# Attention after a group norm: TensorE's side work cut into single matmuls and laid out anew over the sixteen slots of each head

## What is computed

```python
x = x + conv_ref(gn(x), Wq, Wk, Wv, Wproj, bproj)
# conv_ref: q, k, v = xs @ Wq[h], xs @ Wk[h], xs @ Wv[h]
# att = softmax(q @ k.T / 8);  out = att @ v, heads side by side;  out @ Wproj + bproj
```

## Time and profile before

| | |
|---|---|
| median of 3 runs | 4953.66 us (4952.3 to 4955.85) |
| span of the profiled execution | 4946.9 us, 6.8 us under that median |
| TensorE busy | 4705.1 us (95%), 20608 instructions |
| VectorE, ScalarE, GpSimd busy | 2775.5, 2886.6, 2326.6 us |
| mean granted TensorE clock | 0.994 |

### The profile page before, as it was taken

How to read it: one execution, slowest core, us unless ns; L and a number is a source line. 1 busy time by engine, 2 the same in 40 slices (tenths; PEclk the granted TensorE clock), 3 DMA queues, 4 the chain that set the end, 5 groups by cost and what they waited for, 6 DMA issues and landing times.

```text
span 4946.9 us, 73065 instructions
## 1 busy us (share of the span) xinstructions
PE 4705.1 (95%) x20608; PEld 3505.4 (71%) x20608; DVE 2775.5 (56%) x5284; ACT 2886.6 (58%) x5507; POOL 2326.6 (47%) x1837
## 2 busy tenths in 40 slices
PE   7999999999999999999999999999999999999998
PEld 5777767777676776767767677676776767767675
DVE  5655646556465564655646556465564655646454
ACT  4665646556465564655646566464664646656465
POOL 2444545445454454544545445454444545445455
PEclk9999999999999999999999999999999999999999
DMA  2111111111111111111111111211112111111101
GB/s 69 34 37 55 31 53 35 46 46 32 52 34 50 43 34 54 31 53 41 32 54 35 51 41 30 63 28 53 37 30 62 35 49 35 32 61 34 53 23 51
DMA packets 156934, 212.71 MB, mean 43 GB/s; under 512 B 56544, under 2 KB 57568, under 8 KB 156512
## 3 DMA queue, kind: packets, MB, share of 16 engines
q1 hardware_dynamic: 156512, 207.47, 15.0%
HBM read 105.12 MB, written 34.08 MB: 28 GB/s over the span
## 4 chain that ended last, share of the span: by engine, by line
issue 50%; POOL 42%; PE 6%; POOLq 1%; ACT 1%; DVE 0%; DMA 0%; SPq 0%; ACTq 0%; DVEq 0%
POOL prob_l L1031 32%; POOL o L1048 6%; POOL res L1054 3%; PE bank L517 1%; PE bank L561 1%; POOLq L1030 1%; POOL rstd L1023 1%; PE bank L578 1%; PE bank L690 1%; PE bank L692 1%; PE bank L691 1%; PE bank L571 0%; PE bank L572 0%; POOLq L1047 0%; DMA xs<-in_x 0%
## 5 line engine op out<-in xcount | busy, mean ns | idle before, releaser
L1031 POOL TENSOR_TENSOR prob_l<-prob,prob_h 128x512 fp32r<-128x512 f32 x1408 | 1803.5, 1288 | 2470.5 <-ACT prob_h L710 2452.6
L710 ACT ACTIVATE prob<-bank 128x512 f32<-128x512 f32 x2048 | 1237.6, 604 | 1698.6 <-PE bank L572 1579.3
L864 DVE TENSOR_REDUCE smax<-bank 128x1 f32<-128x512 f32 x2048 | 1349.1, 684 | 1012.6 <-PE bank L578 997.8
L710 ACT ACTIVATE prob_h<-bank 128x512 fp32r<-128x512 f32 x2048 | 1236.7, 604 | 198.6 <-PE bank L692 154.9
L690 PE MATMUL bank<-prob_h,vh 128*128 128x512 f32 x2048 | 832.6, 407 | 117.9 <-ACT acc L781 99.3
L578 PE MATMUL bank<-k_hl,q_hh 128*128 128x512 f32 x2048 | 802.5, 436 | 33.6 <-DVE smax L864 30.4
L571 PE MATMUL bank<-q_hh,k_hl 128*128 128x512 f32 x2048 | 824.0, 402 | 0.5 <-ACT prob_h L710 0.5
L572 PE MATMUL bank<-q_lm,k_h 65*128 65x512 f32 x2048 | 813.8, 397 | 0.0
L692 PE MATMUL bank<-prob_l,vh 128*128 128x512 f32 x2048 | 809.6, 395 | 0.0
L691 PE MATMUL bank<-prob_h,vl 128*128 128x512 f32 x2048 | 809.0, 395 | 0.0
L803 DVE TENSOR_TENSOR prob_l<-prob,prob_h 128x512 fp32r<-128x512 f32 x640 | 508.0, 804 | 511.9 <-ACT prob_h L710 511.8
(11 more groups left out here) (58 smaller groups left out, 4393.2 us busy)
## 6 DMA issues: line engine op xcount, KB each, us to landing
xs<-in_x SPq DMA_DIRECT2D x128, 256.0 KB, 2.8
q_hh<-q_hh SPq DMA_DIRECT2D x256, 128.0 KB, 2.2
k_hl<-k_h SPq DMA_DIRECT2D x256, 128.0 KB, 2.4
inv_b<-inv_dram SPq DMA_DIRECT2D x256, 128.0 KB, 2.8
res<-in_x SPq DMA_DIRECT2D x128, 256.0 KB, 2.7
out_x<-res SPq DMA_DIRECT2D x128, 256.0 KB, 2.0
q_lm<-q_lm SPq DMA_DIRECT2D x256, 2.0 KB
den<-acc SPq DMA_DIRECT2D x256, 2.0 KB, 1.7
```

The source lines that it names most:

```text
L710: return nc.scalar.activation(out, ps[ST + bank][:, :], ACT.Exp, scale=SCALE)
L864: nc.vector.tensor_reduce(smax[:, j:j + 1], ps[SM + j % 2][:, :], AX.X, ALU.max).then_inc(rows_used, 1)
L1031: nc.gpsimd.tensor_tensor(prob_l[:, r3, :], prob[:, ring2, :], prob_h[:, r3, :].bitcast(F32), ALU.subtract).then_inc(prob_l_pool, 1)
```

## The change

The side work is counted in single matmuls (`UNITS`), each slot lists its pieces with their bank, and the rows (`"row", n`) stand in the same list, in the order in which they run. q and k are computed one head ahead (`qk`) in heads 0 to 4 and for head 0; `qn` is left in heads 4 and 5 alone, for heads 6 and 7, so the start loses two pieces. Slot 0 now has qk, qn or xt ahead of the value product in every head of the body. `mt` is a transpose. The row matmuls go through four token blocks for one half of the keys, then for the other (`row_of`), so that the first four need only the first half. ScalarE's and VectorE's special rounds of `FIRST` are gone. The tables "single" (head 0 of the first batch, head 3 of the last) and "rows" (head 6 of the last batch), not shown, have two rows each in slots 7 and 8 as well; "single" is "norm" without `mean` and `var`.

```diff
-CHUNKS = {"qk": 4, "qn": 4, "v": 4, "xt": 4, "proj": 4, "mean": 1, "var": 1, "mt": 1}
+UNITS = {"qk": 12, "qn": 12, "v": 24, "xt": 4, "proj": 4, "mean": 1, "var": 1, "mt": 1}
 RES = 3
 BLOCKS = 16
 AHEAD = 3
 POOL_BLOCKS = (1, 4, 5, 6, 7, 8, 9, 11, 12, 13, 15)
...
 WORK = {
-    "plain": ((1, "mt", 1, 0, 1), (10, "mt", 0, 0, 1), (10, "qn", 0, 0, 3), (12, "qn", 1, 0, 3),
-        (12, "qn", 0, 3, 4), (13, "qn", 1, 3, 4)),
-    "values": ((1, "mt", 1, 0, 1), (3, "v", 0, 0, 4), (6, "v", 1, 0, 4), (10, "mt", 0, 0, 1),
-        (11, "qn", 0, 0, 3), (11, "qn", 1, 0, 2), (12, "qn", 0, 3, 4), (13, "qn", 1, 2, 4)),
-    "norm": ((1, "mt", 1, 0, 1), (6, "mean", 0, 0, 1), (9, "var", 0, 0, 1), (10, "mt", 0, 0, 1),
-        (11, "qn", 0, 0, 2), (12, "qn", 0, 2, 4), (12, "qn", 1, 0, 2), (13, "qn", 1, 2, 4)),
-    "tokens": ((0, "xt", 0, 0, 4), (1, "mt", 1, 0, 1), (2, "xt", 1, 0, 4), (3, "xt", 2, 0, 4),
-        (5, "xt", 3, 0, 4), (9, "mean", 1, 0, 1), (10, "mt", 0, 0, 1), (11, "var", 1, 0, 1),
-        (14, "xt", 4, 0, 4)),
-    "next": ((0, "mt", 1, 0, 1), (1, "xt", 5, 0, 4), (2, "xt", 6, 0, 4), (3, "xt", 7, 0, 4),
-        (4, "qk", 0, 0, 4), (5, "qk", 1, 0, 4), (6, "v", 0, 0, 4), (7, "v", 1, 0, 4), (9, "v", 2, 0, 4),
-        (10, "v", 3, 0, 4), (11, "mt", 0, 0, 1), (12, "qn", 0, 0, 4), (13, "qn", 1, 0, 4)),
-    "proj": ((1, "mt", 1, 0, 1), (3, "proj", 0, 0, 4), (4, "proj", 1, 0, 4), (5, "proj", 2, 0, 4),
-        (6, "proj", 3, 0, 4), (8, "proj", 4, 0, 4), (9, "mt", 0, 0, 1), (10, "proj", 5, 0, 4),
-        (11, "proj", 6, 0, 4), (12, "qn", 0, 0, 4), (13, "qn", 1, 0, 4), (14, "proj", 7, 0, 4)),
...
+    "proj": (
+        (("qk", 0, 8, 0), ("mt", 1, 1, 1)),
+        (("qk", 0, 4, 0), ("qk", 1, 2, 1)),
+        (("qk", 1, 6, 1),),
+        (("qk", 1, 4, 1),),
+        (("proj", 0, 4, 0),),
+        (("proj", 1, 2, 1), ("row", 1)),
+        (("proj", 1, 2, 1), ("row", 1)),
+        (("proj", 2, 4, 0), ("row", 1)),
+        (("proj", 3, 4, 1), ("row", 1)),
+        (("proj", 4, 4, 0), ("row", 2)),
+        (("proj", 5, 4, 1), ("row", 2)),
+        (("row", 2), ("mt", 0, 1, 0)),
+        (("proj", 6, 4, 1), ("row", 2)),
+        (("proj", 7, 4, 0), ("row", 2)),
+        (("row", 2),),
+        (),
+    ),
+    "values": (
+        (("qk", 0, 6, 0), ("mt", 1, 1, 1)),
+        (("qk", 0, 6, 0),),
+        (("qk", 1, 6, 1),),
+        (("qk", 1, 6, 1),),
+        (("v", 0, 6, 0), ("row", 1)),
+        (("v", 0, 6, 0), ("row", 1)),
+        (("v", 0, 6, 0), ("row", 1)),
+        (("v", 0, 6, 0), ("row", 1)),
+        (("v", 1, 8, 1), ("row", 1)),
+        (("v", 1, 6, 1), ("row", 2)),
+        (("v", 1, 6, 1), ("row", 1)),
+        (("v", 1, 4, 1), ("row", 2), ("mt", 0, 1, 0)),
+        (("row", 2),),
+        (("row", 2),),
+        (("row", 2),),
+        (),
+    ),
+    "norm": (
+        (("qk", 0, 8, 0), ("mt", 1, 1, 1)),
+        (("qk", 0, 4, 0),),
+        (("qk", 1, 4, 1),),
+        (("qk", 1, 4, 1),),
+        (("qk", 1, 4, 1),),
+        (("row", 1),),
+        (("row", 1),),
+        (("mean", 0, 1, 0), ("row", 2)),
+        (("row", 2),),
+        (("var", 0, 1, 0), ("row", 2)),
+        (("row", 2),),
+        (("mt", 0, 1, 1), ("row", 1)),
+        (("row", 2),),
+        (("row", 2),),
+        (("row", 1),),
+        (),
+    ),
+    "double": (
+        (("qk", 0, 8, 0), ("mt", 1, 1, 1)),
+        (("qk", 0, 4, 0),),
+        (("qk", 1, 6, 1),),
+        (("qk", 1, 6, 1),),
+        (("qn", 0, 2, 0), ("row", 1)),
+        (("qn", 0, 2, 0), ("row", 1)),
+        (("qn", 0, 1, 0), ("row", 1)),
+        (("qn", 0, 1, 0), ("row", 2)),
+        (("qn", 0, 6, 0), ("row", 1)),
+        (("row", 2),),
+        (("qn", 1, 2, 1), ("row", 2)),
+        (("mt", 0, 1, 0), ("qn", 1, 2, 1), ("row", 1)),
+        (("qn", 1, 3, 1), ("row", 1)),
+        (("qn", 1, 5, 1), ("row", 2)),
+        (("row", 2),),
+        (),
+    ),
+    "ahead": (
+        (("qn", 0, 5, 0),),
+        (("mt", 1, 1, 1), ("row", 1)),
+        (("row", 2),),
+        (("row", 1), ("qn", 0, 1, 0)),
+        (("row", 1), ("qn", 0, 1, 0)),
+        (("row", 1), ("qn", 0, 1, 0)),
+        (("row", 1), ("qn", 0, 1, 0)),
+        (("row", 2),),
+        (("qn", 0, 3, 0), ("row", 2)),
+        (("mt", 0, 1, 1), ("row", 1)),
+        (("qn", 1, 3, 1),),
+        (("qn", 1, 3, 1), ("row", 1)),
+        (("qn", 1, 3, 1), ("row", 1)),
+        (("qn", 1, 3, 1), ("row", 1)),
+        (("row", 1),),
+        (),
+    ),
+    "tokens": (
+        (("xt", 0, 4, 0), ("row", 1)),
+        (("mt", 1, 1, 1), ("row", 1)),
+        (("xt", 1, 4, 1), ("row", 1)),
+        (("xt", 2, 4, 0), ("row", 1)),
+        (("row", 1),),
+        (("xt", 3, 4, 1), ("row", 1)),
+        (("row", 1),),
+        (("row", 2),),
+        (("row", 2),),
+        (("mean", 1, 1, 0), ("row", 1)),
+        (("mt", 0, 1, 1), ("row", 1)),
+        (("var", 1, 1, 0), ("row", 1)),
+        (("row", 1),),
+        (("row", 1),),
+        (("xt", 4, 4, 1),),
+        (),
+    ),
+    "next": (
+        (("mt", 1, 1, 0), ("xt", 5, 4, 1)),
+        (("xt", 6, 4, 0),),
+        (("xt", 7, 4, 1),),
+        (("qk", 0, 6, 0),),
+        (("qk", 0, 6, 0), ("qk", 1, 4, 1)),
+        (("qk", 1, 8, 1),),
+        (("v", 0, 12, 0), ("row", 1)),
+        (("v", 0, 12, 0), ("row", 2)),
+        (("v", 1, 10, 1), ("row", 1)),
+        (("v", 1, 14, 1), ("row", 2)),
+        (("v", 2, 12, 0), ("row", 2)),
+        (("v", 2, 6, 0), ("row", 2), ("mt", 0, 1, 1)),
+        (("v", 2, 6, 0), ("row", 2)),
+        (("v", 3, 12, 1), ("row", 2)),
+        (("v", 3, 12, 1), ("row", 2)),
+        (),
+    ),
...
+    "end": ((), (("mt", 1, 1, 1),)) + ((),) * 14,
 }
 
-MAXIMA = {
-    "plain": (0, 0, 2, 1, 1, 1, 2, 0, 1, 2, 1, 2, 1, 1, 1, 0),
-    "values": (0, 0, 2, 1, 2, 0, 2, 0, 1, 1, 2, 2, 1, 0, 2, 0),
-    "norm": (0, 2, 0, 1, 1, 1, 2, 1, 0, 1, 1, 2, 1, 1, 2, 0),
-    "tokens": (0, 1, 1, 1, 1, 1, 1, 1, 1, 2, 1, 2, 1, 2, 0, 0),
-    "next": (0, 0, 0, 0, 0, 0, 0, 2, 2, 2, 2, 2, 2, 2, 2, 0),
-    "proj": (0, 1, 1, 1, 2, 0, 1, 2, 1, 2, 1, 1, 1, 1, 1, 0),
-}
+FRONT = (0, 8)
 
 STAT_SLOTS = ((1, 2, 3, 3), (5, 6, 7, 8))
 
-MEAN_SLOTS = (5, 8)
+MEAN_SLOTS = (6, 8)
...
-FIRST = {
-    "plain": ((0, 8), (), (0, 7, 14)),
-    "values": ((0, 8), (), ()),
-    "norm": ((0, 8), (), ()),
-    "tokens": ((0, 8), (15,), (8,)),
-    "next": ((0, 8), (), (6, 13, 14)),
-    "proj": ((0, 8), (), ()),
-}
...
         return "values"
+    if h == 4:
+        return "double"
+    if h == 5:
+        return "ahead"
     if not has_next:
-        return "plain"
-    return {3: "norm", 6: "tokens", 7: "next"}.get(h, "plain")
...
+def row_of(j):
+
+    group, j = divmod(j, 8)
+    half, t = divmod(j, 4)
+    return 4 * group + t, half
...
-            twice(0, 1, 3)
-            twice(1, 1, 4)
...
                             residual(s, i, s.it)
-                        for t, at in enumerate(PROJ_SLOTS):
-                            if i == at + 1:
+                        for t in range(TT):
+                            if i == s.ends["proj", t] + 1:
...
+                    for u in range(lo, hi):
+                        c, part = divmod(u, 3)
+                        weight, moving = ((wqk_h, xh), (wqk_l, xh), (wqk_h, xl))[part]
+                        last = nc.tensor.matmul(w[:, :], weight[:, c, head, :], moving[:, c, cols],
+                                                start=u == 0, stop=u == 3 * CH - 1)
+                    if hi == 3 * CH:
                         last.then_inc(qk_done, 1)
...
                 elif kind == "mt":
-                    nc.tensor.matmul(w[0:4, 0:P], nmax[:, a * 4:(a + 1) * 4], ident[:, :],
-                                     start=True, stop=True).then_inc(mt_done, 1)
+                    nc.tensor.transpose(w[0:4, 0:P], nmax[:, a * 4:(a + 1) * 4], ident[:, :]).then_inc(mt_done, 1)
...
-                for kind, a, lo, hi in s.slots[i]:
-                    bk, before = s.bank(kind, a)
+                j = sum(s.rows_in(slot) for slot in range(i))
+                for kind, a, lo, hi, bk in s.slots[i]:
+                    if kind == "row":
+                        for _ in range(a):
+                            if j in (0, 4):
+                                half = j // 4
+                                pe.wait_ge(k_split, s.heads(2, 1, half + 1))
+                                pe.wait_ge(qk_twice[(s.k + 1) % 2][half], s.at(16 * NH, 32 * ((s.k + 1) // 2 + 1)))
+
+                            pe.wait_ge(rows_used, s.heads(BLOCKS, 1, j - 1))
+                            row_scores((s.k + 1) % 2, j)
+                            j += 1
+                        continue
+                    before = s.bank(kind, a)[1]
 
                     def wait():
...
-                per_slot = max_blocks(s.h, s.has_next, s.section == "body" and s.k == 8)
-                for j in range(sum(per_slot[:i]), sum(per_slot[:i + 1])):
-                    if j == 0:
-                        pe.wait_ge(k_split, s.heads(2, 1, 2))
```

(22 more changed lines are left out.)

193 lines of the change are left out of this document (111 added, 82 removed).

## The result

The changed kernel takes 5202.64 us, against 4954.76 for the kernel before on the same chip: ratio 1.0499 [1.0484, 1.0513], 5.0% slower. The forecast was 4971, with a range up to 5045. The side was right and the size was not: +248 us where +17 was forecast. The profiled execution spans 5194.1 us.

The account below looks back on a forecast made before the run. TensorE was taken as the bound, with 452 us of its steps lost. Losses after summed to 31.1 us a batch, 497 in all: +45, less 28 for `mt`'s saved pass, gave 4971 us, range 4930 to 5015, wider 4860 to 5045.

Parts of the forecast that it names:

- What is late next: Slots 7 and 8, heads 3 to 6: rows wait for maxima queued behind `prob_l`, delaying value product 8; 8.3 us a batch.
- Tails: Late slots of heads 1 to 4: rows wait for maxima behind `prob_l` or VectorE's other work; 9.1 us a batch.
- Banks at the batch's turn: Heads 7 and 0: transposes, q, k and `mt` 1 wait for banks or for takes; 4.9 us a batch.
- what stays in heads 6 and 0: Remaining waits: head 6 0.5 in slot 0, 0.9 at `xt` 1, 0.4 in slot 14; head 0 0.2 us.
- `mt` and small gaps: Loss kept after the change: 4.8 us a batch around `mt` and 2.0 of small gaps.
- (b): Gaps before and behind `mt`, 0.3 us at each of two a head, 4.8 us a batch, kept as loss.
- rival 2: Faster: the transpose of `mt` does not drain the array; -77 us, 4894; chance 0.07.
- (a): Value product 0 or 8 waits for ScalarE's copy of the bank; 9 us a batch, falling to 0.5.
- Rival 3: Slower: GpSimd's normalisation waits for late reciprocal DMAs in heads 3 and 4, `prob_l` 11 late; +70 us, 5041; chance 0.10.
- Rival 1: Faster: the tails are not there; 174 us, 4797, chance 0.13; half of that, 4884, chance 0.15.

Follow-up runs that it names:

- e3: Changed kernel with VectorE taking the maxima of slot 7's rows ahead of `prob_l` in round 7 (head 6 also round 8), no matmul moved: 5134.59 us.
- e11: e1 with two rows each in slots 7 and 8 of heads 4 and 5, as the changed kernel has in head 5: 4996.07 us.
- e4: Changed kernel with the last projection piece of head 0 in slot 14 instead of slot 13: 5192.10 us.
- e5: Changed kernel with head 5's `qn` 1 in slots 11 to 13, slot 10 empty, and head 7's transposes one slot later: 5132.02 us.
- e9: e3 with the maxima also taken ahead of `prob_l` in rounds 11 and 13 of heads 1, 2 and 3: 5179.48 us.
- e8: e1 with two rows ahead of value product 0 in heads 0 to 5 and two in slot 8 of heads 1, 2, 4, 5: 5076.32 us.
- e6: Changed kernel with each row maximum reading 32 of its 512 columns, order of every queue kept: 5028.39 us.
- e1: The kernel before with `mt` as a transpose and nothing else: 4861.17 us, ratio 0.9821.
- e2: Changed kernel with `mt` as an fp32 matmul again: 5278.34 us, ratio 1.0662.
- e7: Changed kernel with the side work of slot 0 behind value product 0 again, slot 8 as changed: 5247.79 us.
- e10: Changed kernel with the edits of e9, e5 and e4 together: 5080.24 us, ratio 1.0261.

## Why the prediction was wrong in size

Its frame held. The steps' work was counted right: 5075.8 us of steps less 727 of loss leaves 4348 us, against 4372 - 28 = 4344 by the prediction's counts. One size in both is a little low: between undisturbed 512-column matmuls the starts lie 0.231 us apart in either trace, not 0.228, so some 46 us (15276 x 0.003) of the 453 as of the 727 are pace and not waiting, and their difference stays. What went wrong is the loss, 497 us foreseen and 727 measured. Mean loss of the batches in the middle, by the prediction's own steps (a batch is eight steps; in slots where both stand):

| step of the prediction | us a batch, foreseen | measured |
|---|---|---|
| "What is late next", slots 7 and 8 | 8.3 | 9.9 |
| of it heads 3, 4, 5, 6 | 2.7, 0.45, 1.75, 3.4 | 2.6, 0.3, 2.6, 4.4 |
| "Tails", in the slots it named | 9.1 | 10.3 |
| "Banks at the batch's turn", without what stays | 4.9 | 6.5 |
| what stays in heads 6 and 0 | 2.0 | 3.3 |
| `mt` and small gaps | 6.8 | 4.2 |
| places it did not name | 0 | 11.9 |
| sum | 31.1 | 46.1 |

**The slots 7 and 8, the tails and the bank in head 7** stood where the prediction put them. The chain from `acc` over `prob_l` and the maximum to the row is shown in heads 5 and 6 by e3, by e11 in the kernel before, and by the changed kernel's trace, head 5, slot 8 (E = 1869.59):

```profile
1870.91 1.38 DVE L900 TENSOR_TENSOR prob_l<-prob,prob_h 128x512 fp32r<-128x512 f32 x1 [1.81 <-ACT prob_h L813]
...
1872.21 0.68 DVE L962 TENSOR_REDUCE smax<-bank 128x1 f32<-128x512 f32 x1
...
1872.94 0.51 PE L679 MATMUL bank<-k_hl,q_hh 128*128 128x512 f32 x1 [1.57 <-DVE smax L962]
...
1873.77 0.50 PE L679 MATMUL bank<-k_hl,q_hh 128*128 128x512 f32 x1 [0.32 <-DVE smax L962]
...
1874.10 0.39 PE L793 MATMUL bank<-prob_h,vh 128*128 128x512 f32 x1
```

`prob_l` starts at E + 1.32 (1.39 foreseen) but takes 1.38 us, against the 0.92 of the earlier trace rows; so the row comes at E + 3.35 (2.97), the second at 4.18 (3.57), the product at 4.51 (3.80). GpSimd's `o` runs beside it here too, from 1870.46 to 1871.73. Over the batches in the middle this `prob_l` takes 1.37 us in head 5, 1.09 in head 6 and 0.67 in head 3.

The first four terms together come to 30.0 where 24.3 stood: 5.7 us a batch, 90 us in all, inside the third that the forecast allowed them. That they come so near is in part luck. In the tails of heads 1 and 2 slots 12, 13 and 14 lose 1.1, 0.9 and 0.2 us where 0.4, 1.4 and 0.4 were foreseen. The scores' wait for the DMA into `q_lm`, foreseen with 0.2 in those two heads, is not there, and 0.75 each in slot 12 of heads 3 and 4, where none stood. Of the 1.1 us in slot 1 of head 7, put down to `take_rows`, 0.9 is the lower clock.

**The sum of waits was incomplete.** This is the step that failed most: "31.1 us" had no place for 11.9 us a batch, some 185 us, that the changed kernel's trace shows in slots which the prediction passed over:

- The loop's turn, 2.9 us at each of 14 turns. The prediction followed no instruction across it. In the kernel before, eight projection passes of 0.43 in slot 14 keep TensorE's queue ahead of it; e4 put them back and 2.9 us became 0.6.
- Head 5, slots 9 and 10, 2.7 us: 2.2 in slot 10 for a bank whose reader is `take_rows` of `mt` 0, queued behind the take of `qn` 0, and 0.5 of lower clock in slot 9. The prediction walked banks at the batch's turn only; e5 removed the wait, at the price of 0.8 in slot 11.
- Head 7, slot 14, 2.1 us: a row behind a maximum that stands behind `vl` of `v` 2. Heads 1 and 2, slot 9, 1.06 each: the same with `v` 0, as the lines below show. e3 and e9, which move maxima ahead of a `prob_l`, leave both as they were.
- Head 6, slot 9, 1.2, and head 1, slot 0, 0.9: mostly the lower clock.

No run takes the last two groups away; they are read from the trace. Head 1, slot 9 in the changed kernel (ScalarE's cast, VectorE's subtraction behind it, the maxima, the row):

```profile
1733.59 0.77 ACT L832 CAST vh<-bank 128x128 fp32r<-128x128 f32 x4
...
1734.39 0.88 DVE L954 TENSOR_TENSOR vl<-bank,vh 128x128 fp32r<-128x128 f32 x4 [2.12 <-ACT vh L832]
...
1735.20 1.28 DVE L962 TENSOR_REDUCE smax<-bank 128x1 f32<-128x512 f32 x2
...
1735.93 0.50 PE L679 MATMUL bank<-k_hl,q_hh 128*128 128x512 f32 x1 [0.77 <-DVE smax L962]
```

**The lower clock had no term.** Matmuls in stretches at 0.50 lost 16 us of the 128 steps before and 82 after (in the whole execution 54 such stretches, 215 us together, against 13 and 59 us). It is spread over the rows of the table above and is not to be added. e11 shows the link: one edit that made rows wait 104 us longer brought 48 us of lower clock with it. So there each microsecond of added stall cost half again as much. In e8 it rose with the waits, to 91 us. What triggers it is not settled by these runs: e9 has 122 us of it where e3 has 96, with the other losses together as large, and e6 had half the row's waits and still 66.

**(b), "Its narrow output stays, so I keep (b)", was false**, and here the error went the other way. With the transpose the gaps are gone, which was rival 2, at 0.07. e1 gives 89 us and e2 76 for both parts, where the prediction took 28 with bounds 0 and 105. The reason against it, that `xt` has a full-width output, was no evidence against it: the trace of before had no narrow transpose, and `xt` was the nearest row there was. The Trainium skill's rule (TensorE: Matmul & The Clock Gate, Terms) that transpose mode is four times faster for fp32 is not borne out as a pass length here: `mt` goes from two drawn passes of 0.38 together to one of 0.27 drawn, and an `xt` pass has the pitch of 0.11 that each of the two had. Only with the gaps does it come to fourfold, 0.51 us of the stream against 0.12 (e1).

**(a) was right.** It fell from 133 to 11 us of loss (0.7 a batch, 0.5 foreseen), and e7 shows that slot 0's cover is worth 45 us of it. Rival 3 did not happen as such: GpSimd does wait for the reciprocal, 232.6 us in 85 waits (61.6 in 16 before), but TensorE waited for a `prob_l` of GpSimd for 2 us in all. Rival 1, the tails not there, is refuted by slots 12 to 14 of heads 1 and 2, 2.2 us a head as foreseen. e6 shows why "VectorE is busy only 2726 of 4824" was no argument for it.

Added up: 497 foreseen, +90 for the named terms, +185 for the unnamed places, -42 for `mt` and small gaps: 730, against 727 measured.

What stays open: whether the new layout can be mended to pass e1. Its four mends (e10) left it 219 us above. Maxima moved forward made something else late, the DMA into `q_lm` in e9 and the statistics in e3, though in e3 the gain was larger.

## What to carry to other kernels

On an in-order engine a wait is found by walking the queue: for each instruction that is moved, list what stands ahead of the producer it waits for, the reader that must free its bank, the DMA that brings its operand, and what covers the loop's turn, in every slot and not only where the old profile had waits; moving one instruction forward moves another back. Chains that are each sized fairly well still make a sum that is short, since the places one does not think of only add, and here the stalls brought a lower clock along. When a change bundles a sure, local saving with a new layout, measure the saving alone first: here one statement was worth 1.8%, and the layout around it cost 6.9% (1.0499 / 0.9821).

## What the runs showed that was not expected

- An fp32 matmul with a 4-column stationary side holds up the stream before and behind it (starts 0.33, 0.20 and 0.34 us apart); the transpose of the same data does not (0.23, 0.03, 0.32 in e1), nor does a full-width fp32 projection (0.23 behind the matmul before it). With the saved pass that is 0.3 to 0.35 us for each of 256: 89 us by e1, 76 by e2.
- The turn of the loop costs TensorE 2.5 us of idle time (2.9 of loss) where the last matmuls ahead of it are short, and 0.6 where 3.4 us of projection stand there (e4).
- VectorE's `prob_l`, a subtraction of 128x512, takes 0.69 us where GpSimd does nothing beside it (447 of 640 in the changed kernel), and 0.96 on average, up to 1.8, where GpSimd's `o` or another of its operations runs beside it.
- Runs with longer stalls have lower mean granted clocks: 0.996 in e1, 0.985 in e11, 0.980 in the changed kernel, 0.971 in e9 (its profiled execution). The matmuls at the lower level lost 6, 54, 82 and 122 us.
